# Other positions for the feed-forward pieces, norms and free maxima slots in the encoder jobs

## What is computed

```python
x = x + attn_a(layernorm(x))      # 4 encoder layers and a last norm
x = x + ffn(layernorm(x))         # 8 experts, the 2 nearest for each row
x = x + attn_b(layernorm(x))      # one attention with rotary positions
x = x + ffn(layernorm(x))
# one encoder layer of attn_a, 16 heads of 8:
xn = layer_norm(x, ln1_w, ln1_b)
x = x + mha(xn, causal + alibi, in_proj, out_proj)
xn = layer_norm(x, ln2_w, ln2_b)
x = x + gelu(xn @ ffn1_w.T + ffn1_b) @ ffn2_w.T + ffn2_b     # 128 -> 512 -> 128
```

## Time and profile before

| | |
|---|---|
| median of 3 runs | 2632.11 us |
| profiled execution | 2633.4 us, its span 2631.6 us |
| TensorE busy | 2265.3 us, 86% |
| VectorE busy | 1754.1 us, 67% |
| ScalarE busy | 1463.8 us, 56% |
| GpSimd busy | 1039.0 us, 39% |
| mean granted TensorE clock | 0.94 of full speed |

### The profile page before, as it was taken

How to read it: one execution, slowest core, us unless ns; L and a number is a source line. 1 busy time by engine, 2 the same in 40 slices (tenths; PEclk the granted TensorE clock), 3 DMA queues, 4 the chain that set the end, 5 groups by cost and what they waited for, 6 DMA issues and landing times.

```text
span 2631.6 us, 102576 instructions
## 1 busy us (share of the span) xinstructions
PE 2265.3 (86%) x44398; PEld 1386.3 (53%) x44398; DVE 1754.1 (67%) x5525; ACT 1463.8 (56%) x2646; POOL 1039.0 (39%) x1261
## 2 busy tenths in 40 slices
PE   2689999999999999999988888988878778888983
PEld 1345555555555555555545444787644434437872
DVE  6877777787877777787877774532577777752212
ACT  0357777777777777777655556443244434454441
POOL 6334343333433343333445544333234554442135
PEclk9799999999999999999999888999998888889997
DMA  4253333333333433332222210576622221105773
GB/s 115 82 160 103 113 120 118 105 126 98 117 111 105 131 98 126 109 115 92 92 64 72 77 37 18 178 188 202 185 80 67 67 67 59 59 15 184 218 207 107
DMA packets 162531, 288.76 MB, mean 110 GB/s; under 512 B 28504, under 2 KB 116312, under 8 KB 160344
## 3 DMA queue, kind: packets, MB, share of 16 engines
q1 hardware_dynamic: 153696, 264.23, 32.8%
q0 software_dynamic: 8384, 17.97, 2.4%
HBM read 227.33 MB, written 95.96 MB: 123 GB/s over the span
## 4 chain that ended last, share of the span: by engine, by line
PE 61%; DVE 19%; ACT 7%; issue 4%; POOL 3%; SPq 2%; DMA 2%; another core or an unknown queue 1%; POOLq 0%; ACTq 0%; DVEq 0%
PE bank L481 23%; PE bank L647 9%; PE bank L601 9%; DVE mx L1281 6%; PE bank L787 6%; PE bank L797 5%; ACT big L878 3%; PE bank L665 3%; PE bank L488 2%; DVE xn L973 1%; DVE stats L960 1%; ACT OT L884 1%; PE bank L609 1%; DVE xs L1180 1%
## 5 line engine op out<-in xcount | busy, mean ns | idle before, releaser
L878 ACT ACTIVATE big<-bank 128x512 f32<-128x512 f32 x1600 | 919.5, 599 | 695.3 <-PE bank L481 646.6
L1281 DVE TENSOR_REDUCE mx<-bank 128x16 f32<-128x512 f32 (+1 forms) x1440 | 900.8, 652 | 403.3 <-PE bank L609 368.3
L1577 POOL TENSOR_SCALAR_AFFINE_SELECT big<-big 128x768 f32<-128x768 f32 (+1 forms) x640 | 393.7, 639 | 905.7 <-ACT big L878 905.3
L481 PE MATMUL bank<-QS,KS 99*32 99x512 bf16 (+3 forms) x10240 | 645.9, 311 | 44.9 <-ACT big L878 35.7
L601 PE MATMUL bank<-KS,QS 96*32 96x352 bf16 (+15 forms) x10240 | 586.1, 293 | 98.5 <-DVE mx L1281 64.0
L647 PE MATMUL bank<-big,V 128*9 128x256 f32 (+3 forms) x5120 | 454.3, 450 | 19.5 <-POOL big L1577 10.5
L601 PEld LDWEIGHTS bank<-KS,QS 96*32 96x32 bf16 x10240 | 240.1, 98 | 404.7 <-DVE mx L1281 176.2
L481 PEld LDWEIGHTS bank<-QS,KS 99*32 99x32 bf16 x10240 | 216.2, 99 | 218.4 <-ACT big L878 95.2
L609 PE MATMUL bank<-mask_a,ident_b 128*32 128x64 bf16 (+1 forms) x5760 | 303.8, 196 | 0.4 <-issue 0.4
L946 ACT ACTIVATE big<-bank,big 128x256 f32<-128x256 f32 x368 | 151.0, 472 | 246.4 <-PE bank L787 203.1
L787 PE MATMUL bank<-big 128*128 128x256 f32 x736 | 190.8, 405 | 27.9 <-ACT big L931 12.3
(11 more groups left out here) (216 smaller groups left out, 2720.0 us busy)
## 6 DMA issues: line engine op xcount, KB each, us to landing
big<-e_pack SPq DMA_DIRECT2D x92, 578.0 KB
QS<-part_scr SPq DMA_DIRECT2D x480, 96.0 KB
KS<-part_scr SPq DMA_DIRECT2D x480, 96.0 KB
part_scr<-parts SPq DMA_DIRECT2D x80, 384.0 KB
x_rows<-in_alibi SPq DMA_DIRECT2D x47, 384.0 KB, 4.9
y_rows<-in_alibi SPq DMA_DIRECT2D x47, 384.0 KB, 5.4
big<-x_rows SPq DMA_DIRECT2D x92, 128.0 KB
y_rows<-big SPq DMA_DIRECT2D x92, 128.0 KB
```

The costliest lines, as they stand in the source:

```text
L481: last = mm(out[c:c + 32], stationary[:, c:c + 32], moving, start=start, stop=stop)
L878: A(dst, src, ACT.Exp).then_inc(exp_done, 1)
L1281: v.tensor_reduce(mx[:, quad, k, 0:w], src, axis=AX.X, op=ALU.max).then_inc(a_used, 1)
L1577: g.affine_select(out=blocks, in_=blocks, compare_op=ALU.is_ge, fill=0.0, base=0, pattern=[[0, n], [1, P]], channel_multiplier=-1).then_in ...
```

## The change

No instruction is added or taken away; positions and their order change, on all engines, for encoder jobs. Rope jobs keep theirs. In encoder jobs:
- the positions without a maxima chunk are 6, 10, 20 and 39 instead of 9, 19, 29 and 39;
- projections move from 4, 7, 10 to 5, 8, 11, normalisation from 8, 10, 12, 14 to 7, 10, 12, 13;
- value quad 3 goes from 2, 3, 4 to 3, 3, 3, quad 0 from 14, 18, 19 to 18, 20, 20, quad 1 from 29, 29, 29 to 22, 27, 29, quad 2 from 33, 34, 35 to 32, 34, 38;
- first-layer pieces go from 26, 27, 29, 29 to 27, 28, 28, 28, second-layer pieces from 29 (four) to 29, 29, 30, 36, the addition after them from 30 to 39;
- the feed-forward norm goes from 19 and 21 to 18 and 22, the norm for the job three ahead from 33 and 36 to 24 and 27;
- negation and split of the maxima go from 28 to 29, their transposes from 31 to 30, copy and load one position later.

```diff
+WITHOUT = {False: (6, 10, 20, 39), True: (9, 19, 29, 39)}
...
-        def a_chunk(c):
-
-            quad, k = divmod(c, CPQ)
-            return (quad, k, APQ * quad + k) if k < APQ else (quad, None, None)
+        def a_chunk(c, rope_job):
+
+            if (c - SKEW) % CHUNKS in WITHOUT[rope_job]:
+                return None, None, None
+            n = c - sum((pos + SKEW) % CHUNKS < c for pos in WITHOUT[rope_job])
+            return (*divmod(n, APQ), n)
...
TensorE
-                    extras += [(lambda b, j, k=k: project(b, j, k), 2, (4 + 3 * k, 1)) for k in range(2)]
-                    extras += [(project_v, 2, (10, 1))]
+                    extras += [(lambda b, j, k=k: project(b, j, k), 2, (5 + 3 * k, 1)) for k in range(2)]
+                    extras += [(project_v, 2, (11, 1))]
...
+                KTS = ((0,), (1,), (2, 3))
+                if rope_job:
+                    quads = ((0, 0, (14, 18, 19)), (1, 0, (22, 23, 25)), (2, 0, (32, 33, 34)), (3, -1, (2, 3, 4)))
+                    sums = (7, 9, 11, 13)
+                else:
+                    quads = ((3, -1, (3, 3, 3)), (0, 0, (18, 20, 20)), (2, 0, (32, 34, 38)))
+                    sums = (6, 10, 11, 13)
+                for g, rel, at in quads:
+                    extras += [quad_at(g, kts, rel, pos) for kts, pos in zip(KTS, at)]
                 if not rope_job:
-                    extras += [up_at(0, 26), up_at(1, 27), quad_at(1, (0,), 29), quad_at(1, (1,), 29),
-                               up_at(2, 29), up_at(3, 29), quad_at(1, (2, 3), 29)]
-                    extras += [(lambda b, j, t=t: ffn_down(b, j, t), -1, (29, 1)) for t in range(TT)]
...
-                extras += [(lambda b, j, t=t: ot_transposes(b, j, t), -1, (7 + 2 * t, 1)) for t in range(TT)]
-                extras += [(attn_transposes, -1, (15, 1)), (out_project, -1, (17, 1)), (max_transposes, 1, (31, 1))]
+                    extras += [quad_at(1, KTS[0], 0, 22), up_at(0, 27), quad_at(1, KTS[1], 0, 27), up_at(1, 28), up_at(2, 28),
+                               up_at(3, 28), quad_at(1, KTS[2], 0, 29), down_at(0, 29), down_at(1, 29), down_at(2, 30), down_at(3, 36)]
+                extras += [(lambda b, j, t=t: ot_transposes(b, j, t), -1, (pos, 1)) for t, pos in enumerate(sums)]
+                extras += [(attn_transposes, -1, (15, 1)), (out_project, -1, (17, 1)),
+                           (max_transposes, 1, (31 if rope_job else 30, 1))]
                 if not rope_job:
-                    extras += [(ffn_xt, -1, (24, 1))]
+                    extras += [(ffn_xt, -1, (25, 1))]
ScalarE
-                extras = [(xnt, 2, (1, 1))]
+                extras = [(xnt, 2, (1 if rope_job else 2, 1))]
-                    extras += [(lambda b, j, k=k: evac_qk(b, j, k), 2, (5 + 3 * k, 0)) for k in range(2)]
+                    extras += [(lambda b, j, k=k: evac_qk(b, j, k), 2, (6 + 3 * k, 0)) for k in range(2)]
+                for g, rel, pos in ((3, -1, 5 if rope_job else 3), (0, 0, 20), (1, 0, 26 if rope_job else 29), (2, 0, 35 if rope_job else 39)):
+                    extras += [(lambda b, j, g=g: evac_ot(b, j, g), rel, (pos, 1))]
-                    extras += [(ffn_x, -1, (24, 1)), (ffn_gelu, -1, (27, 1))]
+                    extras += [(ffn_x, -1, (25, 1)), (ffn_gelu, -1, (27, 1))]
VectorE
-                extras += [(lambda b, j, t=t: normalise(b, j, t), -1, (8 + 2 * t, 0)) for t in range(TT)]
-                extras += [(add_x, -1, (18, 1)), (negate_split, 1, (28, 1)), (evac_max, 1, (31, 1)),
-                           (lns, 3, (33, 1)), (lna, 3, (36, 1))]
+                extras += [(lambda b, j, t=t: normalise(b, j, t), -1, (8 + 2 * t if rope_job else (7, 10, 12, 13)[t], 0)) for t in range(TT)]
+                extras += [(add_x, -1, (18 if rope_job else 17, 1)), (negate_split, 1, (28 if rope_job else 29, 1)), (evac_max, 1, (31 if rope_job else 32, 1)),
+                           (lns, 3, (33 if rope_job else 24, 1)), (lna, 3, (36 if rope_job else 27, 1))]
-                    extras += [(ffn_lns, -1, (19, 1)), (ffn_lna, -1, (21, 1)), (ffn_add, -1, (30, 1))]
-                    extras += [(lambda b, j, n=n: first_ln(b, j, n), 2, (17 + 8 * n, 1)) for n in range(2)]
+                    extras += [(ffn_lns, -1, (18, 1)), (ffn_lna, -1, (22, 1)), (ffn_add, -1, (39, 1))]
+                    extras += [(lambda b, j, n=n: first_ln(b, j, n), 2, (17 + 6 * n, 1)) for n in range(2)]
GpSimd
-                          (lambda b, j: rsqrt(ln_index(b, j)), 3, (34, 1))]
+                          (lambda b, j: rsqrt(ln_index(b, j)), 3, (34 if rope_job else 25, 1))]
-                    extras += [(lambda b, j: rsqrt(b + j, fln_step, frstd_ready), -1, (20, 1))]
+                    extras += [(lambda b, j: rsqrt(b + j, fln_step, frstd_ready), -1, (19, 1))]
SP
-                          (lambda b, j: load(b, j, 1), 2, (20, 1)), (load_max, 1, (33 if rope_job else 32, 1)),
+                          (lambda b, j: load(b, j, 1), 2, (20, 1)), (load_max, 1, (33, 1)),
```

More of the change, by code:

```diff
@@ L586, in pass_a @@
                 def pass_a(b, j, c):
-                    quad, k, n = a_chunk(c)
+                    quad, k, n = a_chunk(c, rope_job)
                     if k is None:
@@ L726, in attention @@
                 else:
-                    extras += [(lambda b, j, k=k: project(b, j, k), 2, (4 + 3 * k, 1)) for k in range(2)]
-                    extras += [(project_v, 2, (10, 1))]
+                    extras += [(lambda b, j, k=k: project(b, j, k), 2, (5 + 3 * k, 1)) for k in range(2)]
+                    extras += [(project_v, 2, (11, 1))]
                 def up_at(ft, pos):
                     return (lambda b, j: ffn_up(b, j, ft), -1, (pos, 1))
-                def quad_at(g, kts, pos):
-                    return (lambda b, j: pv(b, j, g, kts), 0, (pos, 1))
@@ L735, in attention @@
-                if not rope_job:
-                    extras += [up_at(0, 26), up_at(1, 27), quad_at(1, (0,), 29), quad_at(1, (1,), 29),
-                               up_at(2, 29), up_at(3, 29), quad_at(1, (2, 3), 29)]
-                    extras += [(lambda b, j, t=t: ffn_down(b, j, t), -1, (29, 1)) for t in range(TT)]
[L739 to L743, removed]
@@ L744, in attention, with down_at @@
-                for n, kts in enumerate(((0,), (1,), (2, 3))):
-                    extras += [(lambda b, j, kts=kts: pv(b, j, 3, kts) if b + j < CLEARED else None, -1, (2 + n, 1)),
-                               (lambda b, j, kts=kts: pv(b, j, 3, kts) if b + j >= CLEARED else None, -1, (1 + n, 1))]
-                extras += [(lambda b, j, t=t: ot_transposes(b, j, t), -1, (7 + 2 * t, 1)) for t in range(TT)]
-                extras += [(attn_transposes, -1, (15, 1)), (out_project, -1, (17, 1)), (max_transposes, 1, (31, 1))]
+                def down_at(t, pos):
+                    return (lambda b, j: ffn_down(b, j, t), -1, (pos, 1))
@@ new lines, in quad_at @@
+                def quad_at(g, kts, rel, pos):
+                    return (lambda b, j: pv(b, j, g, kts), rel, (pos, 1))
+                KTS = ((0,), (1,), (2, 3))
[5 more added lines that the diff above has]
+                    sums = (6, 10, 11, 13)
@@ L888, in evac_attn @@
                     A(attnT[:], bankR[:], ACT.Copy).then_inc(attnT_ready, 1)
-                extras = [(xnt, 2, (1, 1))]
+                extras = [(xnt, 2, (1 if rope_job else 2, 1))]
                 if not rope_job:
-                    extras += [(lambda b, j, k=k: evac_qk(b, j, k), 2, (5 + 3 * k, 0)) for k in range(2)]
-                extras += [(lambda b, j: evac_ot(b, j, 3) if b + j >= CLEARED else None, -1, (4, 1)),
-                           (lambda b, j: evac_ot(b, j, 3) if b + j < CLEARED else None, -1, (5, 1))]
-                extras += [(lambda b, j, g=g, at=at: evac_ot(b, j, g), 0, (at, 1)) for g, at in enumerate((20, 26 if rope_job else 30, 35 if rope_job else 36))]
+                    extras += [(lambda b, j, k=k: evac_qk(b, j, k), 2, (6 + 3 * k, 0)) for k in range(2)]
+                for g, rel, pos in ((3, -1, 5 if rope_job else 3), (0, 0, 20), (1, 0, 26 if rope_job else 29), (2, 0, 35 if rope_job else 39)):
+                    extras += [(lambda b, j, g=g: evac_ot(b, j, g), rel, (pos, 1))]
                 extras += [(evac_attn, -1, (15, 1))]
```

## The result

The changed kernel took 2559.54 us (median of 4 runs, 2555.85 to 2574.79), beside 2629.93 us for the kernel before on the same chip: a ratio of 0.9747, 95% interval 0.9722 to 0.9772. The profiled execution took 2560.24 us against 2633.4. The forecast was 2575 us in a range of 2548 to 2624; the sign and the range held, the forecast's own narrower range (from 2560) was missed by half a us. The profiled executions lie 73 us apart, the medians 70, where 57 was forecast.

The account below looks back on a forecast made before the run. TensorE was the engine to keep fed, losing 2.6 us a plain period to waits. Gains of 22 x 1.9 and 6 x 2.5, 56.8 us, took the profiled 2633.4 to 2576.6, so a median of 2575 us, range 2548 to 2624.

Parts of the forecast that it names:

- Plain period: Encoder period without routing work, 22 counted: 1.9 us gained of 2.6 lost, after taking off 0.5 and 0.2.
- new waits and tight places: Plain period: 0.3 us lost in positions 0 to 17, 0.2 at exponential 20, 0.2 for tight places at 28 to 30.
- the period without stalls: Plain period with TensorE's four losses, 2.6 us in all, gone: 43.1 us.
- Routing period: Six encoder periods with routing beside them: 3.2 us of VectorE work moves into idle time; gain 2.5, bounds 0 and 4.
- From 30 to 39 VectorE gives up 2.6 us: Positions 30 to 39: norm and statistics leave VectorE (1.55 + 1.06), so most of 0.7 us lost ahead of 742.14 goes.
- Little to win in 0 to 17: Positions 0 to 17: none of the four losses lies there, a new wait can arise; 0.3 us lost.
- Cover at 30: Position 30: the maxima's split ends at 16.9, TensorE arrives for their transposes at 17.0; cover only 0.1 us.
- Exponential 20: Position 20: exponential 20 waits for the end of value quad 0, since both share a buffer; 0.2 us.
- The port shared by VectorE and GpSimd: Position 39: the moved addition meets GpSimd's clearing, adding up to 1.2 us to VectorE, about 1 us reaching TensorE.
- second rival: Positions 39 to 20: half comes back as new waits, gain 0.8 per plain and 1.7 per routing period; 2604 us, chance 0.23.
- The first: Whole encoder period: nearly all of the loss goes, 2.5 us per plain and 3.5 per routing period; 2556 us, chance 0.13.
- the third: Position 30: TensorE waits for the split of the maxima, 1.0 us slower per plain period; 2654 us, chance 0.11.

Follow-up runs that it names:

- down_only: Kernel before with only the second-layer pieces moved to 29, 29, 30, 36 and their addition to 39: 2601.08 us, ratio 0.9884.
- down_back: Changed kernel with all four second-layer pieces back at 29 and the addition after them at 30: 2602.06 us, ratio 0.9872.
- free_back: Changed kernel with the positions without a maxima chunk back at 9, 19, 29, 39: 2559.73 us, ratio 0.9723.
- quad0_early: Changed kernel with the last two pieces of value quad 0 at 19 instead of 20: 2555.17 us, ratio 0.9711.
- start_and_evac: Changed kernel with early norms back, second first normalisation at 25, expert packing spread over jobs 1 to 4, quad 0 and its evacuation ahead of exponential 20: 2549.38 us.
- best: start_and_evac with the packing copies cut by expert, four small ones at 34 of each of jobs 1 to 8: 2552.82 us, ratio 0.9699.
- norms_back: Changed kernel with the norm for the job three ahead back at 33, 34 and 36: 2586.62 us, ratio 0.9812.
- norms_only: Kernel before with only the norm for the job three ahead at 24, 25, 27 and first normalisations at 17 and 23: 2617.60 us, ratio 0.9939.
- norms_down: Kernel before with the edits of norms_only and down_only together: 2601.22 us, ratio 0.9879.
- values_too: Kernel before with norms, second-layer pieces, feed-forward norm, value quads 0 and 1 and first-layer pieces as in the changed kernel: 2586.29 us, ratio 0.9826.

## Why the prediction was right, and where it was off
- *Engine and direction* held: TensorE was to be kept fed, and the long waits were for VectorE and ScalarE at 18 to 40. In the period shown the reordering removed those for VectorE and left two for ScalarE.
- *The total* is nearer than its terms: the plain periods gave 19 us more than forecast and the routing periods 10 more, and the ends, forecast at nothing, took 14 back.
- *Plain period, 1.9 us forecast, 2.8 measured.* Two terms were mis-sized, and the runs don't divide the 0.9 us between them. One is the 0.7 us taken off for new waits and tight places. The other is the loss, 2.6 us by counting stretches of the chain, and with it the period without stalls, 43.1: the changed kernel runs at 42.82 with two waits left. I treated the chain's runs on TensorE as work, but recorded busy time fell by 1.05 us with the order alone.
- *Routing period, 2.5 forecast with 4 as the upper bound, 4.3 measured.* The forecast priced only what leaves the stretch behind the second-layer block, mainly the norms, and that held: they are worth 2.5 us alone and 2.6 undone. It gave nothing for the rest. The second-layer pieces alone make a routing period 1.3 us shorter (57.7, down_only), and undoing them 1.9 longer (56.6, down_back). Each figure is an average over six periods of one execution, and kernels that differ little from the changed one spread from 54.7 to 55.6 us (free_back, quad0_early, start_and_evac, best), so 4 against 4.3 is not much of a miss. TensorE's granted clock is also below full there: 0.84 to 0.96 in the six periods before the change, 0.88 to 1.00 after it.
- *Periods at the ends, forecast nothing.* The start lost 7.5 us. norms_back's first load, 6.5 us earlier, and start_and_evac's both point to the norms: the first normalisations, each with a wait for GpSimd, stood with them between 17 and 27. TensorE's clock came on top. Ten microseconds each around the first load, in the columns of the earlier trace rows, the changed kernel twice and start_and_evac:

```profile
170.00:180.00 10.00, 6.50 (x104) 3.11 (x104) 8.71 (x36) 3.77 (x6) 3.27 (x5) 0.66 0.83 248
180.00:190.00 10.00, 8.91 (x108) 3.29 (x108) 6.41 (x23) 4.62 (x6) 1.01 (x1) 0.66 1.05 304
```
```profile
170.00:180.00 10.00, 10.00 (x232) 5.83 (x232) 8.60 (x42) 9.14 (x14) 2.57 (x4) 1.00 0.41 153
```

  With TensorE waiting for VectorE the granted clock is 0.66 in both stretches, so the lower of its two levels (1.2 GHz) for some two thirds of the time, and TensorE gets through 104 and 108 matmuls where start_and_evac, at 1.00, does 232. A group of eight score matmuls takes 0.43 us in the changed kernel's chain there, 0.22 in a plain period. In the kernel before, the clock was 0.92 and 1.00 in these stretches. How the 7.5 us divide between the waits and the clock is not shown.
- *Part by part, in plain periods.* "From 30 to 39 VectorE gives up 2.6 us" is worth nothing by itself (norms_only, norms_down) and 1.15 once everything else is in place. (The 6 us that the prediction counts for VectorE there leave out the addition moved to 39; with it they are 7.4 beside 8.5.) "Little to win in 0 to 17" was wrong: values_too shows that the wait goes to 9 to 14 when 18 to 25 is mended. No part of the set that was tried closes them all, and the undone parts (1.15 + 1.70 + 0.30) add up to more than the whole gain of 2.89.
- *Cover at 30.* I put the transposes ahead of the third second-layer piece; in TensorE's list that piece stands first. Measured cover 0.46 us for 0.1.
- *Exponential 20.* I charged 0.2 us to its wait for quad 0. ScalarE on the chain at 20 to 22, one of the signs of being wrong, did appear, for 1.25 us. The chain shows the evacuation behind it and quad 1 at 22 instead; taking both waits apart won 0.09 us.
- *The port shared by VectorE and GpSimd.* The two do meet at 39, but in plain periods it is GpSimd that waits. Timelines of the changed kernel, a plain period (718 us) and a routing one (1404 us):

```profile
718.00 0.69 DVE L1357 TENSOR_TENSOR xs<-xs,fp_sb 128x512 f32<-128x512 f32 x1
...
1404.44 0.69 DVE L1357 TENSOR_TENSOR xs<-xs,fp_sb 128x512 f32<-128x512 f32 x1
1405.05 0.85 DVE L1072 TENSOR_TENSOR s<-s 128x32 f32<-128x32 f32 x1
```
```profile
718.46 1.31 POOL L1583 TENSOR_SCALAR_AFFINE_SELECT big<-big 128x768 f32<-128x768 f32 x2 [2.94 <-ACT big L885]
...
1404.53 1.68 POOL L1583 TENSOR_SCALAR_AFFINE_SELECT big<-big 128x768 f32<-128x768 f32 x2 [2.94 <-ACT big L885]
```

VectorE's addition starts first and keeps its 0.69 us (0.691 to 0.694 in all 32 jobs); the clearing, 1.22 us elsewhere, takes 1.31 and 1.68, and in plain periods no instruction waits for it. In the routing period VectorE pays after all, one instruction later: its small addition at 1405.05, beside the second half of that clearing, took 0.85 us, where the median of this line is 0.19. In the case of the earlier trace rows GpSimd was at work already when VectorE's addition began at 1403.43: a row scatter from 1402.81 to 1403.76, then its own addition to 1405.07. The Trainium skill ("SBUF — State Buffer", "Who interferes with whom") says that whoever issues first has the pair for the whole instruction: by that rule, these rows agree on who waits. The time added to the clearing (0.09 and 0.46 us) is less than its overlap with the addition (0.23 and 0.60). I had let the cost fall on VectorE, and with it 1 us a plain period in the second rival; there it fell on an engine with room.
- *Rivals.* The first (nearly all of the loss goes, 2556 us, given 0.13) came nearest to the total. The second and the third did not happen.

## What to carry to other kernels
When engines that run fixed lists meet at several places in a period, mending one place shows little, because the wait moves to the next. Judge a part by undoing it in the finished set as well as by doing it alone (1.15 against 0.06 us here), and in each kind of period: the same edit was worth 2.5 us either way where routing work lay beside it. Measure the distance of a once-per-period instruction in the trace: it told differences of 0.1 us in 43 apart where the totals of one kernel scattered by 10 us and more in 2600. A periodic schedule has a start of its own: what fits the steady period cost 7 us in the first ones, part of it through a lower clock.

## What the runs showed that I had not expected
- Recorded busy time of TensorE is not a constant of the instructions: 43.52 and 42.47 us for a period of the same ones at the same clock.
- A load of the keys that is off the chain elsewhere held it for 8.6 and 12.4 us when issued just after bulk copies in DRAM, whether these were four large ones or thirty-two small ones.
- The table load before Gelu waits for TensorE as its activation does: it began 0.26 us after ScalarE was free, when first-layer piece 0 came one position later, and so can't be hidden in that wait.
